# Retention tower on one core: values product in 32-column tiles, scores on two 64-row halves, bias inside the accumulation, a norm moved to ACT, new points of order

## The reference

```
Q, K, V  = per-head projections of layernorm(X)       # 4 heads of 32
A        = einsum('bnsd,bntd->bnst', Q, K) * D        # D: causal decay
Y        = einsum('bnst,bntd->bnsd', A, V)
Yn       = ((Y - mean) / sqrt(var + EPS)) * gnw + gnb # per token and head
Y1       = (G * sigmoid(G) * Yn) @ WO + X
X        = gelu(layernorm(Y1) @ w1 + b1) @ w2 + b2 + Y1
```

## Time and profile before

| | |
|---|---|
| median of 3 runs | 2769.51 us (2760.56 to 2775.77) |
| profiled execution, its own time | 2767.15 us |
| its span | 2765.3 us |
| PE busy | 2505.9 us, 91% |
| DVE / POOL / ACT busy | 2042.8 / 1984.1 / 1557.8 us (74 / 72 / 56%) |
| mean granted TensorE clock | 0.972 |
| chain that ended last | PE 68%, POOL 14%, DVE 7%, issue 6% |

### The profile page before, as it was taken

The page is one execution under the profiler, slowest core; times in us unless marked ns, Lnnn a source line. Parts: engine busy times, 40 slices in busy tenths (PEclk is TensorE's granted clock), DMA queues, the critical chain, the costliest instruction groups (busy, mean ns, idle before and its releaser), DMA issues.

```text
span 2765.3 us, 49055 instructions
## 1 busy us (share of the span) xinstructions
PE 2505.9 (91%) x16336; PEld 2123.8 (77%) x16336; DVE 2042.8 (74%) x6261; ACT 1557.8 (56%) x4733; POOL 1984.1 (72%) x2286
## 2 busy tenths in 40 slices
PE   0499999999999999999999999999999999977775
PEld 0378888888888888888888888888888888865553
DVE  5368888888787878787878887887888797764443
ACT  0156666666666666666666666666666666542332
POOL 4787777777777787868787777777787854445666
PEclk9799999999999999999999999999999999988897
DMA  4521110202021202111111112020211000003443
GB/s 158 203 72 58 61 63 27 95 25 98 26 95 29 95 27 73 49 61 63 60 62 61 62 41 81 25 98 27 95 29 33 27 17 22 7 8 108 141 133 105
DMA packets 107320, 181.25 MB, mean 66 GB/s; under 512 B 23748, under 2 KB 46406, under 8 KB 106960
## 3 DMA queue, kind: packets, MB, share of 16 engines
q1 hardware_dynamic: 73296, 110.87, 11.8%
q0 software_dynamic: 33792, 67.45, 8.3%
HBM read 89.54 MB, written 90.78 MB: 65 GB/s over the span
## 4 chain that ended last, share of the span: by engine, by line
PE 68%; POOL 14%; DVE 7%; issue 6%; another core or an unknown queue 2%; DMA 1%; ACT 1%; SPq 1%; POOLq 0%; ACTq 0%; DVEq 0%
PE psum L1097 61%; POOL grams L568 6%; PE psum L1116 4%; POOL gr L607 3%; PE psum L1165 3%; POOL side_rstd L586 1%; POOL routed_rows L627 1%; POOL rstd L579 1%; DVE hid L945 1%; DMA grams<-expert_w 1%; DVE side_n L874 1%; ACT sq L693 1%; PE psum L1111 1%; DVE xn L860 0%
## 5 line engine op out<-in xcount | busy, mean ns | idle before, releaser
L568 POOL DMA_INDIRECT grams<-gram_table,idx_all x768 | 780.0, 1016 | 195.5 <-issue 184.5
L1097 PE MATMUL psum<-xT,lw 128*128 128x256 f32 x1920 | 487.9, 385 | 11.9 <-ACT xT L674 8.5
L1097 PE MATMUL psum<-lw,hid 128*128 128x129 f32 x3072 | 409.6, 276 | 1.7 <-ACT hid L712 1.7
L579 POOL TENSOR_TENSOR rstd<-ss,con 128x2 f32<-128x2 f32 x320 | 230.3, 720 | 251.4 <-ACT squares L667 230.8
L1097 PE MATMUL psum<-qm,qkT 128*128 128x512 f32 x768 | 371.8, 607 | 23.6 <-DVE kv L934 21.0
L1097 PEld LDWEIGHTS psum<-lw,hid 128*128 128x128 f32 x3072 | 381.6, 192 | 9.0 <-ACT hid L712 3.8
L1097 PE MATMUL psum<-V,hid 128*128 128x32 f32 x3072 | 383.0, 269 | 5.7 <-issue 3.2
L1097 PEld LDWEIGHTS psum<-V,hid 128*128 128x128 f32 x3072 | 375.1, 192 | 12.8 <-issue 12.1
L1097 PEld LDWEIGHTS psum<-xT,lw 128*128 128x128 f32 x1920 | 339.7, 193 | 50.2 <-ACT xT L674 13.0
L712 ACT ACTIVATE hid<-psum,par 128x256 f32<-128x256 f32 x768 | 317.9, 474 | 49.8 <-PE psum L1097 44.3
L607 POOL TENSOR_TENSOR gr<-ms,con 128x8 f32<-128x8 f32 x192 | 324.6, 1691 | 16.0
(11 more groups left out here) (176 smaller groups left out, 4832.7 us busy)
## 6 DMA issues: line engine op xcount, KB each, us to landing
routed_rows<-pad SPq DMA_DIRECT2D x265, 264.0 KB
grams<-expert_w SPq DMA_DIRECT2D x44, 321.0 KB
grams<-gram_table,idx_all POOLq DMA_INDIRECT x768
grams<-routed_rows SPq DMA_DIRECT2D x44, 264.0 KB
xb<-x SPq DMA_DIRECT2D x32, 256.0 KB
lw<-layer_w SPq DMA_DIRECT2D x1, 2503.5 KB, 12.0
routed_rows<-row,slot POOLq DMA_INDIRECT x128
con<-consts SPq DMA_DIRECT2D x1, 1339.5 KB, 6.0
```

Source lines behind the costliest of these rows:

```text
L568: pool.indirect_dma_start(grams[s][:, g, c, :], None, gram_table, bass.IndirectOffsetOnAxis(ap=idx_all[:, g, at:at + 1], axis=0))\
L579: pool.tensor_tensor(rstd[s][:, CS[h]], ss[s][:, CS[h]], const("half")[:, 0:2], ALU.pow)\
L1097: return pe.matmul(dst, lhsT, rhs, start=start, stop=stop)
```

## The change

Six edits, with constants and semaphores to match:
1. **Values product.** The operands change places: 32 columns of `V` are stationary and the 128 columns of `A` move. The output `Y` is transposed (a head's 32 values on 32 partitions, tokens along the columns), and each head's product goes to its own 32 output partitions. The state product changes places in the same way and both of its instructions now stand ahead of the eight.
2. **Scores.** ACT makes two masked copies of the queries (even and odd heads) in place of four. Heads 0 and 1 lie on rows 0 to 63, heads 2 and 3 on rows 64 to 127; each chunk has two products with 64 contraction rows and 256 columns, one into bank `a`, one into bank `b`.
3. **Norm of Y.** The sum of squares per head is a product on PE with 4 columns per chunk, DVE adds EPS (and reads PSUM), POOL only takes the power. ACT spreads the result over 128 columns, PE transposes that in place of `Y`, ACT applies the gain, and DVE multiplies it with `Y` and then adds the bias and multiplies with the gate.
4. **ffn_b2** is added by PE: two bf16 products of 129 columns close the accumulation of the down product. The bias is split into three bf16 parts in the setup. `Y1b` on POOL is gone.
5. **Second norm** of the layer (`norm_apply` on `Y1`): two ACT instructions of 128x128 in place of one DVE instruction of 128x256.
6. **Points of order** now differ by layer, and the starts of the streams and of the later gathers are tables.

The core of the diff:

```diff
-START = (0, 28.01)
-HLAG = 12.18
+LATER_GATHERS = (4.35, 14.81, 25.34, 26.48, 63.86, 73.15, 88.73, 102.67, 104.01, 105.74, 111.61, 119.84)
+LAGS = ((0, 12), (28.34, 40.35))
...
                 k = it * LAYERS + l
-                yield -2.74
+                yield (-26.05, 2.65, -0.25)[l]
                 if l:
                     norm_rstd(it, s, 2 * l - 1, h)
                 n = CH * HEADS // 2
                 c = slice(h * n, (h + 1) * n)
-                yield 16.96
+                yield (25.03, 24.99, 22.41)[l]
                 pool.wait_ge(y_ms[s], nth(k, 2, h))
-                link(pool.tensor_scalar(ms[s][:, c], ms[s][:, c], EPS, 1.0, ALU.add, ALU.mult))
                 pool.tensor_tensor(gr[s][:, c], ms[s][:, c], const("half")[:, 0:n], ALU.pow).then_inc(y_r[s], 1)
 
             def feed(it, s, l, h):
                 k = it * LAYERS + l
-                yield -2.95
+                yield (2.1, 2.11, 0.45)[l]
                 norm_rstd(it, s, 2 * l, h)
-                yield 4.41
-
-                pool.wait_ge(y1_s[s], nth(k, 2, h))
-                pool.tensor_tensor(Y1b[s][:, CS[h], :], Y1[s][:, CS[h], 0:WIDE],
-                                   param("ffn_b2", l, WIDE).unsqueeze(1).to_broadcast([P, 2, WIDE]), ALU.add)\
-                    .then_inc(y1b_s[s], 1)
...
+            def norm_apply(s, h, src, scale):
+                for c in half_chunks(h):
+                    last = act.activation(xn[s][:, c, :], src[s][:, c, 1:WIDE], ACT.Copy, scale=scale[s][:, c:c + 1])
+                last.then_inc(n_out[s][h], 1)
+
...
-                for n in range(HEADS):
-                    last = act.activation(qm[s][:, h, n, :], bank_b(s, h)[:, 0:2 * P], ACT.Copy,
-                                          scale=const("heads")[:, n * HD:n * HD + 1])
+                for j in range(2):
+                    last = act.activation(qm[s][:, h, j, :], bank_b(s, h)[:, 0:2 * P], ACT.Copy,
+                                          scale=const("parity")[:, j:j + 1])
...
+                yield (24.69, 23.97, 21.92)[l]
+                n = CH * HEADS // 2
+                act.wait_ge(y_r[s], nth(k, 2, h))
+                act.activation(xn[s][:, CS[h], :].rearrange("p c (n d) -> p (c n) d", d=HD),
+                               gr[s][:, h * n:(h + 1) * n].unsqueeze(2).to_broadcast([P, n, HD]), ACT.Copy)\
+                   .then_inc(y_rb[s], 1)
+                yield (26.49, 25.15, 23.12)[l]
+                act.wait_ge(rT_y[s], nth(k, 2, h))
+                act.activation(zp[s][:, TS[h]], bank_b(s, h)[:, 0:2 * P], ACT.Copy,
+                               scale=param("gn_w", l)).then_inc(z_a[s], 1)
+                yield (29.84, 29.58, 28.64)[l]
...
-                yield 1.18
+                yield (-112.47, 1.55, 0.62)[l]
+                act.wait_ge(n_rstd[s][h], nth(it, OWN, 2 * l))
+                norm_apply(s, h, Y1, rstd)
...
+            def split_bias2():
+
+                rest = param("ffn_b2")
+                for n in range(3):
+                    link(dve.tensor_copy(bias2_part[n][:, :], rest))
+                    if n < 2:
+                        link(dve.tensor_tensor(bias2_rest[:, :], rest, bias2_part[n][:, :], ALU.subtract))
+                        rest = bias2_rest[:, :]
+                link(dve.tensor_scalar(bias2[:, :], bias2_part[0][:, :], eye[:, 0:1], None, ALU.mult))
+                for n in (1, 2):
+                    link(dve.scalar_tensor_tensor(bias2[:, :], bias2_part[n][:, :], eye[:, n:n + 1], bias2[:, :],
+                                                  ALU.mult, ALU.add))
+                link(dve.tensor_scalar(below_three[:, :], const("vocab"), 3.0, None, ALU.is_lt))
+                dve.tensor_scalar(three_bf[:, :], ones_bf[:, :], below_three[:, :], None, ALU.mult)
...
-                yield 14.88
-                dve.wait_ge(y_sq[s], nth(k, 2, h))
-                dve.tensor_reduce(ms[s][:, h * n:(h + 1) * n], sq[s][:, cs, :].rearrange("p c (n d) -> p (c n) d", d=HD),
-                                  axis=AX_X, op=ALU.add).then_inc(y_ms[s], 1)
-                yield 18.66
-                dve.wait_ge(y_r[s], nth(k, 2, h))
-                dve.tensor_tensor(xn[s][:, cs, :].rearrange("p c (n d) -> p (c n) d", d=HD),
-                                  a[:, 0:2 * P].rearrange("p (n d) -> p n d", d=HD),
-                                  gr[s][:, h * n:(h + 1) * n].unsqueeze(2).to_broadcast([P, n, HD]), ALU.mult)\
-                   .then_inc(y_n[s], 1)
-                yield 22.65
+                yield (21.73, 20.86, 19.3)[l]
+                dve.wait_ge(ms_p[s], nth(k, 2, h))
+                dve.tensor_scalar(ms[s][:, h * n:(h + 1) * n], a[:, 2 * P:2 * P + n], EPS, None, ALU.add)\
+                   .then_inc(y_ms[s], 1)
+                yield (27.33, 25.08, 24.29)[l]
                 dve.wait_ge(z_a[s], nth(k, 2, h))
-                dve.tensor_tensor(zp[s][:, ts], zp[s][:, ts], sw[s][:, ts], ALU.mult).then_inc(z_s[s], 1)
-                yield 24.88
+                link(dve.tensor_tensor(zp[s][:, ts], a[:, 0:2 * P], zp[s][:, ts], ALU.mult))
+                dve.scalar_tensor_tensor(zp[s][:, ts], zp[s][:, ts], param("gn_b", l), sw[s][:, ts], ALU.add, ALU.mult)\
+                   .then_inc(z_s[s], 1)
...
-                yield -1.13
-                dve.wait_ge(n_rstd[s][h], nth(it, OWN, 2 * l))
-                norm_apply(s, h, Y1, rstd)
-                yield 7.7
+                yield (12.21, 11.6, 13.84)[l]
                 dve.wait_ge(ff_p[s], nth(k, 2, h))
-                dve.wait_ge(y1b_s[s], nth(k, 2, h))
-                dve.tensor_tensor(X[s][:, cs, 0:WIDE], wide(bank_a(s, h)), Y1b[s][:, cs, :], ALU.add).then_inc(x_s[s], 1)
+                dve.wait_ge(y1_s[s], nth(k, 2, h))
+                dve.tensor_tensor(X[s][:, cs, 0:WIDE], wide(bank_a(s, h)), Y1[s][:, cs, 0:WIDE], ALU.add).then_inc(x_s[s], 1)
...
                 for i in range(2):
-                    mm(chunks((a, b)[i]), qkT[s][:, h, 1, i, :], qm[s][:, h, :, chunk(i)]).then_inc(sc_p[s], 1)
-                yield 13.05
+                    for r in range(2):
+                        part = slice(64 * r, 64 * r + 64)
+                        last = mm((a, b)[r][:, i * 2 * P:(i + 1) * 2 * P].rearrange("p (j q) -> p j q", j=2),
+                                  qkT[s][part, h, 1, i, :], qm[s][part, h, 0:2, chunk(i)])
+                        if i == 1:
+                            last.then_inc(sc_p[s], 1)
+                yield (17.72, 16.04, 15.49)[l]
 
                 pe.wait_ge(kv_s[s], nth(k, 2, h))
+                pe.wait_ge(sc_s[s], nth(k, 4, 2 * h + 1))
+                for c in half_chunks(h):
+                    if c:
+                        mm(a[:, chunk(c % 2)], kv[s][:, c - 1, :], qkT[s][:, h, 0, c % 2, :], c < 3, False)
                 for c in half_chunks(h):
                     i = c % 2
-                    pe.wait_ge(sc_s[s], nth(k, 4, c))
-                    if c:
-                        mm(a[:, chunk(i)], qkT[s][:, h, 0, i, :], kv[s][:, c - 1, :], True, False)
                     for n in range(HEADS):
-                        last = mm(a[:, i * P + n * HD:i * P + (n + 1) * HD], A[s][:, h, i, n, :],
-                                  V[s][:, c, n * HD:(n + 1) * HD], c == 0, c == 0 or n == HEADS - 1)
+                        d = slice(n * HD, (n + 1) * HD)
+                        last = mm(a[d, chunk(i)], V[s][:, c, d], A[s][:, h, n // 2, 2 * i + n % 2, :], False, i == 1)
                 last.then_inc(y_p[s], 1)
-                yield 20.53
-                pe.wait_ge(y_n[s], nth(k, 2, h))
+                yield (20.34, 18.3, 19.18)[l]
+                pe.wait_ge(y_sq[s], nth(k, 2, h))
+                for c in half_chunks(h):
+                    last = mm(a[:, 2 * P + c % 2 * HEADS:2 * P + (c % 2 + 1) * HEADS], sq[s][:, c, :],
+                              const("heads").rearrange("p (n d) -> p n d", d=HD)[:, :, 0])
+                last.then_inc(ms_p[s], 1)
+                yield (23.95, 23.04, 21.92)[l]
+                pe.wait_ge(y_rb[s], nth(k, 2, h))
                 if l == 0 and it:
                     pe.wait_ge(rT_s[s], nth(it - 1, 2, h))
                 if l == 1 and it:
                     pe.wait_ge(r_slot[s], nth(it - 1, 2, h))
                 if l == 2 and it + 1 < pairs:
                     pe.wait_ge(h0_s[s], nth(it + 1, 2, h))
-                half_transposes(b, xn[s], h).then_inc(yT_p[s], 1)
-                yield 24.01
+                half_transposes(b, xn[s], h).then_inc(rT_y[s], 1)
...
                         pe.wait_ge(f_s[s], nth(k, 4, 2 * h + f // 2))
                     for i in range(2):
-                        last = mm(wide(a)[:, i, :], hid[s][:, h, f, chunk(i)], w2[:, f, :], f == 0 and i == 0,
-                                  f == FB - 1 and i == 1)
+                        mm(wide(a)[:, i, :], hid[s][:, h, f, chunk(i)], w2[:, f, :], f == 0 and i == 0, False)
+                for i in range(2):
```

(31 more changed lines are left out.)

94 lines of the change are left out of this document (47 added, 47 removed).

## The result

The changed kernel takes **2654.07 us** in the median of 4 runs (2650.43 to 2660.86), the kernel before 2769.46 on the same chip: a ratio of 0.9588, 95% interval 0.9555 to 0.9621, 115 us less. The forecast was 2676. The profiled execution took 2655.26 us, its span is 2653.3.

The account below looks back on a forecast made before the run. The prediction took PE to bound the half-layers; -140 (values), -123 (scores), +79 (sum of squares), +21 (bias) and +72 (changes of tiling) sum to -91 us, from 2767.15 to 2676 us. Range 2510 to 2800.

Parts of the forecast that it names:

- PE bounds the steady part: Over the 192 half-layers PE, busy 293 of 300 us, sets the pace; time it saves leaves the total nearly one for one.
- Values, forecast -140 as couples: Values product on PE: neighbouring heads' products overlap in pairs, 1.70 to 0.97 us per half-layer, a gain of 140 us.
- Rival 1: Values and scores on PE: four column tiles and both row halves run at once, -237 us, 2530 us; chance 22%.
- nine slots: Values block on PE: eight two-instruction products, started in order and overlapping in pairs, take 9 x 0.108 = 0.97 us.
- Scores, forecast -123: Scores on PE: eight 256-column instructions on two row halves take 1.08 us against 1.72, a gain of 123 us.
- the fifth slot: Scores block on PE: overlapping in pairs, eight instructions were given five slots of 0.216 us, 1.08 us together.
- Changes of tiling, forecast +72 at 0.10: PE's array is divided anew 721 times, at 0.10 us each, adding 72 us.
- Rival 2: Each change of tiling on PE costs 0.285 us by emptying and exposed weight loads: 2809 us, slower; chance 14%.
- Sum of squares and bias: New PE products: four sum-of-squares instructions per half-layer add 79 us, bf16 bias instructions at 0.055 us add 21 us.
- All else at 0: State product, work moved between ACT, DVE and POOL, and setup were costed at 0; PE's block times hide the moves.
- ACT's balance: ACT loses two query copies, gains two norm instructions and a spreading copy: +38 us, costed at 0.
- rival 3: Shorter PE blocks expose waits for ACT and POOL; PE loses 17 us in 300, giving 2752 us; chance 12%.

Follow-up runs that it names:

- double_sq: The changed kernel with the product for the sums of squares issued twice: 2576.03 us, 62 us slower than the changed kernel.
- head_outer: The changed kernel with the two loops of the values product exchanged, heads outside and chunks inside: 2515.07 us, 0.9264 of the kernel before.
- more_switches: The changed kernel with the values block split by a state product in half 1, 192 more changes of tiling: 2530.23 us, 14 us more.
- scores_full: The changed kernel with scores at full height as before, with four masked query copies: 2650.59 us, 134 us slower than the changed kernel.
- values_only: The changed kernel with the scores, bias and second-norm edits all undone: 2702.85 us, 0.996 of the kernel before.

## Why the prediction was right, point by point

- **PE bounds the steady part**: right on the other chips (292 of 300), and 7 tenths of added PE work came through (double_sq). On the first chip it was 282.55.
- **Values, forecast -140 as couples**: mis-sized. Four stream at once; in streaming alone the block fell from 1.66 to four slots, 0.43, 235 us. Rival 1 had this right. The failing step is "nine slots": four were measured, and head_outer shows that the reason given for nine, a start in the written order, does not hold. The Trainium skill, "TensorE: Matmul & The Clock Gate", section "Packing small matmuls", has distinct tiles run concurrently; the trace agrees, with starts 7 ns apart for fp32 too, where the page says about 4.
- **Scores, forecast -123**: four slots of 0.216 and not five. Streaming alone saves 158. The row as a whole fell by 0.64, 123 us, which is the forecast's figure by luck: changes of tiling fill the place of the fifth slot.
- **Changes of tiling, forecast +72 at 0.10**: mis-sized. The emptied array is right (0.10 ahead of the values block), but behind a block some more is lost, which I take for exposed weight loads. What the budget of the other chips has beyond streaming is 0.153 in the values row, 0.184 in the scores, 0.023 in the bias and 0.188 in the neighbours, 0.55 per half-layer, over 3.76 changes 0.146 each, +105 us. more_switches has 0.165. Rival 2 had named the exposed loads, but its 0.285 was too dear.
- **Sum of squares and bias**: +79 and +21 forecast, +81 and +22 measured (0.421, and 2 x 0.057 in scores_full; where the scores are divided too, a change of tiling adds 0.023).
- **All else at 0**: wrong, and the largest gap in the reasoning. With PE in a budget alone, values_only should have gained 235 - 81 - 56 = 98 us (384 changes at 0.146 are 56). It gained 12, and the 80 of idle time above are most of the difference. Of the moves off PE that were costed at nothing, undoing the one of the bias costs at most 44 us, that of the norm at most 72, and the order of the gathers 296. They keep PE fed once its blocks are short; what they give without the values product was not run. ACT's balance was taken at +38 us. The groups' busy times give +52 (`qm` lost 142, the two new pieces brought 214, `zp` lost 20), but ACT as a whole was busy only 6 us more, and the lengths of all its rows sum to 1964.6 us against 1960.9: it got hardly any load, only new waits.
- **The sum on the other chips**: -235 - 158 + 81 + 22 + 105 - 15 (idle) = -200, where 198 and 201 were measured and 91 forecast.
- **The sum on the first chip**: PE's rows -157 and idle +55, together -103 over the counted stretch. This is rival 3's size of loss, PE idle 17 us in 300, but not its cause: between 500 and 1900 us PE waits 29 us for ACT's `xn` on this chip and 26 on another, while its waits for "issue" (16 us) and for DVE's `kv` (14 us) stand in the changed kernel's trace on the first chip alone. It lands at 2654, near my 2676: the figure was met by luck, because two errors, an overlap and an off-PE cost both too small, cancel. On the other chips the same forecast of 3.3% stands against 7.3%, and rival 1's 237 us is nearer than its 91.

**What stays open** is why the first chip's waits are longer. In its trace the other engines and PE itself wait for things that the profile can't name. PE, and ACT around one such place:
```profile
1230.50 0.44 PE L1138 MATMUL psum<-con,xn 128*128 128x128 f32 x2
1230.78 1.48 PE L1119 MATMUL psum<-lw,xT 128*128 128x256 f32 x8
1232.09 0.60 PE L1119 MATMUL psum<-xT,lw 128*128 128x256 f32 x2
1232.52 0.38 PE L1138 MATMUL psum<-con,xn 128*128 128x128 f32 x2
1234.55 0.48 PE L1119 MATMUL psum<-xT,lw 128*128 128x256 f32 x1 [1.65 <-issue]
```
```profile
1233.93 0.56 ACT L677 ACTIVATE xT<-psum,par 128x256 f32<-128x256 f32 x1 [3.60 <-remote]
```
ACT starts its copy 3.0 us after the recorded end of the transposes at 1230.94. Between 500 and 1900 us such waits of ACT's `xT` sum to 36.6 us (19 times); the changed kernel on the other chips has none. All such waits of PE, ACT and DVE, "remote" and "issue" together, are 115 us in these 1400 of the changed kernel on the first chip, 83 in the kernel before there, and at most 1.1 in either kernel on the other chips. So they belong to the chip and not to the change. I have no run that shows the cause, and a guess would be a story.

## What to carry to other kernels

When blocks on the bounding engine shrink by a large factor, price two things apart: what streams (here four tiles at once, 0.11 us for four fp32 instructions) and what each new division of the array costs (0.15 us). Then ask of every "free" move off that engine whether its cover lasts: here the edit with the largest saving on PE gave 12 of 200 us with three of the others undone. About 94 of the other 188 are PE's own, by the scores; most of the rest is idle time that went when POOL and ACT could deliver in time. Move the small work and the order of the long transfers together with the big edit, and measure on more than one chip before an effect of a few per cent is called the kernel's.

## What was unexpected of the hardware

- Tiles fill whatever the order of the loops: head_outer is equal within 0.1% (2515.07 and 2516.22).
- fp32 instructions on four 32-column tiles start 7 ns apart. The two of a product are on one tile, so a four must be one of each head; that PE looks past the waiting second instruction is inferred from this and from the 13 ns of head_outer; no row names it.
- 55 us, 2%, lie between chips for the kernel before, and 138 us, 5%, for the changed one, with equal durations of single instructions and a granted clock of 0.99 to 1.00 in the steady part.
- The points of the twelve gathers of a stream in POOL's list, with nothing else moved, are worth 296 us of 2516; moving all of them 2.0 earlier costs 50.
